# Pre-sums on GpSimd in all 60 same-class steps, with the taps, logit planes and value pieces moved between steps

## The reference, cut to what matters

```
x_pool = x.reshape(b, h, STRIDE, w, STRIDE, c).mean(axis=(2, 4))
a = x_pool @ W_a + b_a                                  # 28 x 28 windows, 12 heads, 9 x 9
a = softmax(a * scale)
out = einsum('bnpqk,bnpkd->bnpqd', a, v_un)             # v_un: 3 x 3 patches of x @ W_v
folded = folded.at[:, ii, jj, :].add(out)               # fold back to 56 x 56
y = folded[...] @ W_o + b_o
x = x + y
x = x + conv3x3_depthwise(gn(x), signs of w)
```

## Time and profile before

| | |
|---|---|
| median of 3 runs | 5262.09 us (5259.7 to 5266.69) |
| profiled execution, its own time | 5268.83 us |
| its span | 5266.6 us |
| mean granted TensorE clock | 0.834 |
| busy: PE, DVE, GpSimd, ACT | 4189.2, 4192.7, 3362.1, 2035.5 us |

### The profile page before, as it was taken

The page is one execution under the profiler, slowest core; times in us unless marked ns, Lnnn a source line. Parts: engine busy times, 40 slices in busy tenths (PEclk is TensorE's granted clock), DMA queues, the critical chain, the costliest instruction groups (busy, mean ns, idle before and its releaser), DMA issues.

```text
span 5266.6 us, 58011 instructions
## 1 busy us (share of the span) xinstructions
PE 4189.2 (80%) x13632; PEld 2149.8 (41%) x13632; DVE 4192.7 (80%) x4747; ACT 2035.5 (39%) x2881; POOL 3362.1 (64%) x3628
## 2 busy tenths in 40 slices
PE   4877887888887788887788877888877888878884
PEld 2434444444443444443444443444434444434442
DVE  5688787788787888877887878888778878788876
ACT  4334443244443344433444433444433444324421
POOL 5766766666666666666666656666666676666661
PEclk7988888888888888888888888888888888888876
DMA  1111111101111101111011111011111111110110
GB/s 38 37 35 25 46 42 37 46 18 41 46 33 46 37 23 46 46 33 46 21 39 46 35 44 45 15 46 46 33 46 25 34 46 39 40 46 15 44 37 19
DMA packets 126229, 195.55 MB, mean 37 GB/s; under 512 B 14248, under 2 KB 115464, under 8 KB 122472
## 3 DMA queue, kind: packets, MB, share of 16 engines
q1 hardware_dynamic: 97384, 155.50, 12.3%
q10 hardware_dynamic: 28672, 38.55, 2.4%
HBM read 39.22 MB, written 38.54 MB: 15 GB/s over the span
## 4 chain that ended last, share of the span: by engine, by line
PE 47%; DVE 25%; issue 18%; ACT 5%; DVEq 1%; DMA 1%; POOL 1%; ACTq 0%; SPq 0%; POOLq 0%; PEldq 0%; PEld 0%
PE acc L764 25%; PE bc L744 10%; DVE strip L657 9%; DVE prod L607 6%; PE side L709 6%; DVE top L633 3%; PE side L703 3%; DVE top L637 3%; DVE X L621 2%; ACT X L446 2%; PE side L715 1%; PE side L721 1%; DMA out<-tok_out 1%; ACT strip L540 1%; DVEq L249 1%
## 5 line engine op out<-in xcount | busy, mean ns | idle before, releaser
L764 PE MATMUL acc<-prod,wo 96*96 96x392 f32 x5312 | 2537.6, 580 | 340.6 <-DVE X L621 338.5
L607 DVE TENSOR_TENSOR prod<-bc,VAL 96x784 f32<-96x784 f32 x2048 | 1965.0, 964 | 805.5 <-PE bc L744 723.8
L369 POOL TENSOR_TENSOR prod<-prod 96x392 f32<-96x392 f32 x1440 | 1457.5, 1016 | 1328.0 <-DVE prod L607 1323.5
L744 PE MATMUL bc<-stack,sel 96*96 96x392 f16 x4608 | 1312.9, 381 | 525.4 <-DVE prod L607 508.8
L764 PEld LDWEIGHTS acc<-prod,wo 96*96 96x96 f32 x5312 | 987.0, 190 | 889.4 <-DVE X L621 502.9
L744 PEld LDWEIGHTS bc<-stack,sel 96*96 96x96 f16 x4608 | 589.9, 140 | 1473.9 <-DVE prod L607 824.0
L657 DVE SCALAR_TENSOR_TENSOR strip<-XP,sg,strip 96x448 f32<-96x448 f32 x1568 | 1062.9, 678 | 157.8 <-ACT strip L540 139.4
L351 POOL TENSOR_TENSOR att<-att,top 108x420 f32<-108x420 f32 (+1 forms) x576 | 590.8, 1044 | 162.3 <-DVE top L633 162.3
L439 ACT ACTIVATE att<-side,ba 108x420 f32<-108x420 f32 (+1 forms) x576 | 339.8, 595 | 915.5 <-PE side L709 868.2
L357 POOL TENSOR_TENSOR att<-att,top 108x420 f32<-108x420 f32 (+1 forms) x576 | 591.0, 1045 | 42.1 <-ACT top L473 42.1
L709 PE MATMUL side<-pooled,wa 96*108 96x392 f32 (+1 forms) x1152 | 508.4, 554 | 33.3 <-ACT pooled L498 20.5
(11 more groups left out here) (56 smaller groups left out, 2232.3 us busy)
## 6 DMA issues: line engine op xcount, KB each, us to landing
stack<-part SPq DMA_DIRECT2D x192, 275.3 KB
stack<-part SPq DMA_DIRECT2D x192, 256.9 KB
tok_in<-in_x SPq DMA_DIRECT2D x32, 1176.0 KB, 8.5
out<-tok_out ACTq DMA_DIRECT2D x224, 168.0 KB, 4.7
stack<-part SPq DMA_DIRECT2D x192, 30.5 KB
stack<-part SPq DMA_DIRECT2D x192, 28.5 KB
X<-in_L_conv_W_a SPq DMA_DIRECT2D x1, 364.5 KB
ACC<-select SPq DMA_DIRECT2D x1, 144.0 KB
```

Source lines behind the costliest of these rows:

```text
L369: nc.gpsimd.tensor_tensor(p[:, 0, :], p[:, 0, :], p[:, 1, :], ALU.add).then_inc(pre_added, 1)
L607: nc.vector.tensor_tensor(prod[:, g % PRODUCTS, :, :].rearrange("c a (i j) -> c a i j", j=WIN), b, v, ALU.mult).then_inc(prod_ready, 1)
L744: last = nc.tensor.matmul(bc[g % 2][0:CH, a, 0:UNIT], sel[:, which, :], stack[h][:, qi, ki * TAPS + kj, si:si + HALF, sj:sj + WIN], start= ...
L764: last = nc.tensor.matmul(acc[0:CH, 0:UNIT], wo[:, :], prod[:, g % PRODUCTS, a, :], start=first, stop=s == LAST[c] and (g in PRE or t == 2 ...
```

## The change

Only the table `AT` changes. All 60 same-class steps have the pre-sum. In the steps of the class additions there are no taps, and the taps are spread over the steps between, two in most of those; the centre taps of the last two strips are at steps 43 and 49 instead of 42 and 48. Some logit planes and value pieces are at other steps: in the first half planes 2, 3 and 4, which were together at step 21, are at 20, 21 and 22, and three planes are then read at step 22; in the second half the planes 4, 5 and 6 move from step 48 to step 47.

```
-    "not pre": (0, 3, 8, 9, 10, 14, 15, 16, 22, 28, 33, 39, 46, 51, 54),
+    "not pre": (),
-    V: ((27, 30, 33, 33), (62, 63, 65, 67)),
-    LOG: ((19, 19, 21, 21, 21, 22, 22, 23, 23), (39, 39, 42, 43, 48, 48, 48, 51, 53)),
+    V: ((27, 30, 33, 34), (62, 63, 65, 66)),
+    LOG: ((19, 19, 20, 21, 22, 22, 22, 23, 23), (39, 40, 42, 44, 47, 47, 47, 51, 54)),
-    "normed": (18, 33),
+    "normed": (18, 34),
-    "centred": (12, 18, 24, 30, 36, 42, 48),
-    "taps": (13, 13, 14, 15, 15, 16, 17, 17, 19, 19, 20, 21, 21, 22, 23, 23, ...
+    "centred": (12, 18, 24, 30, 36, 43, 49),
+    "taps": (13, 13, 14, 14, 16, 16, 17, 17, 19, 19, 20, 20, 21, 21, 23, 23, ...
```

More of the change, by code:

```diff
@@ L85 @@
     "rimmed": 10,
-    "centred": (12, 18, 24, 30, 36, 42, 48),
-    "taps": (13, 13, 14, 15, 15, 16, 17, 17, 19, 19, 20, 21, 21, 22, 23, 23, 25, 25, 26, 27, 27, 28, 29, 29, 31, 31, 32, 33, 33, 34, 35, 35, 37, 37, 38, 39, 39, 40, 41, 41, 43, 43, 44, 45, 45, 46, 47, 47, 49, 49, 50, 51, 51, 52, 53, 53),
+    "centred": (12, 18, 24, 30, 36, 43, 49),
+    "taps": (13, 13, 14, 14, 16, 16, 17, 17, 19, 19, 20, 20, 21, 21, 23, 23, 25, 25, 26, 26, 27, 28, 28, 29, 31, 31, 32, 32, 33, 33, 35, 35, 37, 38, 39, 40, 40, 41, 42, 42, 44, 44, 45, 45, 46, 46, 48, 48, 50, 50, 51, 51, 52, 52, 53, 53),
 }
```

## The result

The changed kernel takes 5569.6 us (median of 4 runs, 5553.23 to 5582.05) against 5263.8 us for the kernel before on the same chip: a ratio of 1.058, with an interval of 1.0546 to 1.0613. It is 306 us slower, 9.9 us for each image, and outside the predicted range. The direction was right; the predicted 133 us are less than half of what came.

A forecast was written before the change was run, and what follows sets the result against it. It took an image's time as DVE's own work plus its waits, with no engine full; 1.7 - 1.2 + 3.8 = 4.3 us an image, times 31 is 133 us, added to 5262.1 gives 5395 us; range 5295 to 5485.

The forecast's parts named there:

- Term 1: Steps 0 to 25: a first pre-sum waiting for product 0 and a later product 16 cost +1.7 us an image.
- I therefore give no gain for the matmuls and no further loss: Steps 16 to 25: single `add_up` gains nothing, late pre-sums lose nothing more; product 25 stays 1.7 us late.
- Term 2: Steps 26 to 47: a single `add_up` at step 39 and product 44 filling a wait give -1.2 us an image.
- Term 3: Steps 47 to 50: two successive waits, 10.2 us against 6.45 before, cost +3.8 us an image.
- Part (b): Step 50: DVE stands 4.9 us for the last centre tap, behind the last `HIGH`, which waits for `MUL` 8.
- Part (a): Step 47: product 48 waits 5.3 us for half an `add_up`, three planes and four maps on PE.
- rival (3): Worse: PE at half clock in steps 51 to 57 and 15 to 20, about 2 us more an image, 5457 us; chance 0.22.
- Neither is a term of the sum: Whole image: GpSimd's added 15.2 us and PE's saved 9.8 us do not count in bulk; the order decides.
- 1.2 GHz in this stretch and 2.4 GHz elsewhere: PE's clock in the kernel before: half only at 2767 to 2777 us of the profile, full in the rest.
- Rival (2): Faster: GpSimd keeps up and single `add_up` removes waits, -3.0 us an image, 5169 us; chance 0.15.

The follow-up runs named there:

- e7: The changed kernel with 12 unread matmuls on PE in step 13, in place of standing ahead of the pre-sum of step 10: 5489.2 us.
- e3: The changed kernel with the last centre tap at step 48 instead of 49, ahead of the last `HIGH` on ACT: 5357.0 us.
- e1: The kernel before with the 15 added pre-sums and nothing else of the change: 5392.4 us.
- e2: The changed kernel without the 15 added pre-sums, all moved instructions kept: 5486.5 us.
- e12: The kernel before with seven more pre-sums, in steps 22, 28, 33, 39, 46, 51 and 54: 5329.0 us.
- e14: e12 with four unread matmuls of 96 columns added on PE in each of its seven steps with an added pre-sum: 5284.4 us.
- e5: The changed kernel without the 15 added pre-sums and with the last centre tap back at step 48: 5284.6 us.
- e4: The changed kernel with its planes 4, 5 and 6 back at step 48 instead of 47: 5571.4 us.
- e13: The kernel before with maps of five steps computed repeatedly into their own bank, and unread matmuls ahead of steps 42, 46 and four class additions: 5125.1 us.

## Why the prediction was right or wrong, point by point

**Term 1, steps 0 to 25: +1.7 predicted, +5.2 measured.** The order part was right in size. The first pre-sum waits for product 0 (2.27 us), ACT's last `EXP` of the half waits 0.53 us for GpSimd's last `SUB`; product 16 waits 3.02 us, where 1.5 or more was asked. In e7, where the mean clock of steps 13 to 19 is 0.95, the two stretches have 8.15 us of waits against 6.45 before: +1.7, the term as predicted, 1.36 of it ahead of product 16. That it fits so well is in part luck: the 0.4 us by which the first taps were to be late did not come (they start 26.8 us behind product 0 in both traces), and there are 0.4 us more ahead of products 1 to 12. The missing 3.5 us are the half clock. The step that failed is the sentence "I therefore give no gain for the matmuls and no further loss". I had the pre-sums of 10 and 11 arriving just as PE wants them, and took that for harmless. The pre-sum of 10 ended 26.8 us after product 0, where my sum has 27.3, so its time was right. But PE had nothing left ahead of it and stood for 2.48 us, and what followed was not a delay of that size but seven steps at 1.2 GHz.

**Term 2, steps 26 to 47: -1.2 predicted, -1.4 measured** (steps 26 to 46). The wait ahead of the taps of steps 43 and 44 fell from 1.24 to 0.41, and the 0.52 ahead of product 43 went.

**Term 3, steps 47 to 50: +3.8 predicted, +4.7 measured.** Part (b) was 4.94 against 4.9, behind the `HIGH` that waited 5.13 us for `MUL` 8, and e3 takes it away with one number. Part (a) was 6.21 against 5.3. In the image shown it is 6.65: the `add_up` took 1.41, the planes 3.92 (3.9 in my sum) and the maps 1.22, which I had at about 0.65 by taking the full clock back before them; and the 0.6 that I took off for the addition's end was not there, as PE began only when it had ended. The term named +4.4 as its upper end. Product 48 waits and product 49 doesn't, as written.

**Steps 51 to 57: 0 predicted, +1.3 measured.** Clock again: steps 55 to 57 are at 0.74 in the image shown and at 0.67 to 0.72 in nearly all images of e1, where they were at 1.00. The 5 us of standing in step 50, which rival (3) gave as the reason, are not needed for it: e1 doesn't have them and has +1.9 here, and e2, which has them without the added pre-sums, has +0.3. Rival (3) had named both this stretch and the return at steps 15 to 20, and was priced at 2 us for an image. Against the forecast the two places cost 3.5 and 1.3 us. So what (3) foresaw, the half clock in these two places, came at more than twice its price and with a chance of 0.22 where it should have led.

**The step that failed for the whole** is "Neither is a term of the sum", for the 9.8 us taken from PE. They are a term with the sign reversed: e1 takes away all of them, moves nothing else, and loses 122 us, and e12 takes 14 of the 30 records away with no wait for a pre-sum that matters and loses 60 us. Empty matmuls win 45 of these back (e14), though for the most part in other steps. The profile had hinted at it, with a granted clock of 0.84 before and DVE standing after most class additions. I read that clock wrongly: "1.2 GHz in this stretch and 2.4 GHz elsewhere" can't be, since 0.84 over 160.44 us is some 51 us at the half clock in each image, and the stretch that I had looked at is 10 us long. Steps 58 to 63 were at 0.56 before. I used the half clock to price what I had already placed in step 48 and did not ask where else it was or would appear.

By what I cited: the Trainium skill, "TensorE: Matmul & The Clock Gate", section "HAM oscillation — how this bites in real kernels", says that idle gaps between bursts of matmuls bring the slow clock back. These runs agree: 2.48 us of standing before seven steps of 21.6 us at 0.53, and e7's 15.8 us at 1.00 with that gap filled. I gave that rule a rival and no share of the sum.

Rival (2) has a slip that changed nothing: the savings that it lists (1.7, 1.4 and 1 to 1.3 us) make 4.1 to 4.4 us, and it takes 3.0.

**What stays open.** Which part of e2 makes the 2.4 us of waits at steps 58 to 63, which e5 no longer has. Why e12's losses in steps 12 to 25 and 51 to 57 mostly stay in e14, and how much of the last 15 us is GpSimd's. And the effects do not add: e4's gain is given back elsewhere, and a whole image alternates with the next, so I can say what each edit does in its company, not what it is worth alone.

## What to carry to other kernels

Before taking work from TensorE, see where it will then stand, and price the matmuls behind that wait at the half clock; where nothing waits for TensorE's end, fewer matmuls can be a loss. When an instruction is moved to an in-order queue such as ACT's, read which instruction stands ahead of it and when that one's input is ready: one centre tap behind a `HIGH` cost 213 us here, and all 15 pre-sums by themselves 122. Where the waits of TensorE can't be shortened, repeat work into a bank that is free anyway: this took 2.8% off here.

## What was not expected of the hardware

- Making PE do more made the kernel faster: 4416 matmul records more (e13, 18048 against 13632), 144 us less.
- The loss from the slow clock comes far from its cause. In e12, whose first added pre-sum is in step 22, waits grew by 1.1 us behind products 12, 15 and 18 together, and the mean clock fell from 0.834 to 0.812; in e4 an edit at step 48 lengthened steps 13 to 19 of the next image.
- The same two records of one `add_up` matmul took 0.82 us in e7 at 2960.89 and 1.62 us at 3007.22 in the changed kernel, while GpSimd's pre-sum took 1016 ns in both kernels although 480 more of them ran beside DVE.
